# Attention and quantised feed-forward on one core: the second inverse root moved behind the head sums, squares per tile, part of the maximum taken early, bias row moved behind the first quantised tiles

## The reference, cut to what matters

```
n1  = layernorm(x)                       # inverse root of the variance: the first inverse root
q   = rope(n1 @ Wq), k = rope(ctx @ Wk), v = ctx @ Wv      # 16 query heads in 4 groups, 4 kv heads of 32
a   = mean over heads of softmax(q k / sqrt(32)) v
x1  = x + a @ Wo
n2  = layernorm(x1)                      # the second inverse root
i_scale = max(|n2|) / 127                # one number over all 64 batches
out = (clip(round(n2 / i_scale)) @ ternary(W).T) * w_scale * i_scale + bias
y   = x1 + out
```

## Time and profile before

| | |
|---|---|
| median of three runs | 1318.34 us (1316.42 to 1319.36) |
| profiled execution, its own time | 1320.26 us |
| its span, first to last instruction | 1318.4 us |
| mean granted TensorE clock | 0.989 |
| busy: PE, DVE, ACT, POOL | 96%, 89%, 78%, 60% of the span |
| first part, steady | about 150 to 950 us |
| change between the parts | about 950 to 978 us |
| second part | 978 us to the end |

### The profile page before, as it was taken

The page is one execution under the profiler, slowest core; times in us unless marked ns, Lnnn a source line. Parts: engine busy times, 40 slices in busy tenths (PEclk is TensorE's granted clock), DMA queues, the critical chain, the costliest instruction groups (busy, mean ns, idle before and its releaser), DMA issues.

```text
span 1318.4 us, 36698 instructions
## 1 busy us (share of the span) xinstructions
PE 1269.2 (96%) x9848; PEld 1087.7 (82%) x9911; DVE 1174.6 (89%) x2644; ACT 1026.7 (78%) x2338; POOL 794.8 (60%) x1536
## 2 busy tenths in 40 slices
PE   6897999999999999999999999999969999999998
PEld 5787999999999999999999999999935555555554
DVE  4876899999999999999999999999968888888887
ACT  3454788888888888888888888888857888888886
POOL 3564888888888888888888888888820000000000
PEclk9998999999999999999999999999979999999999
DMA  8674345465555555555555452322108999999945
GB/s 268 172 212 129 104 148 192 146 191 154 183 158 178 162 174 162 174 169 168 174 163 181 155 169 75 102 77 100 37 0 334 400 401 399 397 401 402 406 202 223
DMA packets 100815, 265.18 MB, mean 201 GB/s; under 512 B 49705, under 2 KB 65769, under 8 KB 72114
## 3 DMA queue, kind: packets, MB, share of 16 engines
q1 hardware_dynamic: 100786, 264.86, 58.5%
HBM read 139.64 MB, written 125.17 MB: 201 GB/s over the span
## 4 chain that ended last, share of the span: by engine, by line
PE 86%; DVE 6%; DMA 3%; issue 2%; SPq 1%; ACT 1%; POOL 1%; DVEq 0%; POOLq 0%; ACTq 0%
PE bank L1245 18%; PE bank L1165 17%; PE bank L1213 13%; PE bank L1135 8%; PE bank L1200 8%; PE bank L1186 6%; PE bank L1236 4%; PE bank L1176 4%; PE bank L1243 3%; PE bank L1155 2%; PE bank L1147 2%; DMA x_sb<-in_ctx 1%; PE bank L1062 1%; DMA k_scr<-x_sb 1%; DVE cT_parts L752 1%
## 5 line engine op out<-in xcount | busy, mean ns | idle before, releaser
L1245 PE MATMUL bank<-wT,x_sb 128*128 128x512 f16 x1024 | 263.9, 380 | 3.5 <-issue 0.2
L1165 PE MATMUL bank<-wqs,xT_sb 128*128 128x128 f32 x2048 | 260.8, 281 | 0.4 <-ACT xT_sb L639 0.3
L717 ACT ACTIVATE x_sb<-bank,mean,cols 128x512 f32<-128x512 f32 x256 | 196.2, 775 | 67.5 <-PE bank L1245 67.3
L1165 PEld LDWEIGHTS bank<-wqs,xT_sb 128*128 128x128 f32 x2048 | 239.1, 192 | 7.1 <-ACT xT_sb L639 0.7
L1213 PE MATMUL bank<-v_blk,pT_sb 103*128 103x136 f32 x1536 | 199.0, 279 | 0.3 <-ACT pT_sb L681 0.3
L927 DVE SCALAR_TENSOR_TENSOR x_sb<-x_sb,mv_sb,bank 128x512 f32 (+1 forms) x256 | 180.0, 745 | 14.9 <-PE bank L1176 5.1
L1213 PEld LDWEIGHTS bank<-v_blk,pT_sb 103*128 103x128 f32 x1536 | 190.6, 190 | 0.5 <-ACT pT_sb L681 0.5
L1245 PEld LDWEIGHTS bank<-wT,x_sb 128*128 128x128 f16 x1024 | 100.6, 98 | 106.8 <-issue 1.7
L690 ACT ACTIVATE sq_sb<-x_sb 128x512 bf16 (+1 forms) x256 | 161.6, 631 | 18.7 <-DVE x_sb L927 1.4
L897 DVE TENSOR_REDUCE amax<-x_sb (+1 forms) x128 | 156.0, 1219 | 21.5 <-DVE bn_sb L888 6.3
L1002 DVE TENSOR_TENSOR x_sb<-x_sb 128x512 f32 (+1 forms) x256 | 164.8, 685 | 1.2 <-ACT x_sb L717 1.2
(11 more groups left out here) (125 smaller groups left out, 2566.8 us busy)
## 6 DMA issues: line engine op xcount, KB each, us to landing
out_y<-x_sb SPq DMA_DIRECT2D x112, 1024.0 KB, 7.2
x_sb<-in_x SPq DMA_DIRECT2D x64, 1024.0 KB, 6.4
x_sb<-out_y SPq DMA_DIRECT2D x48, 1024.0 KB, 9.1
x_sb<-in_ctx SPq DMA_DIRECT2D x38, 256.0 KB, 2.8
k_blk<-k_scr SPq DMA_DIRECT2D x256, 19.2 KB, 5.5
k_scr<-x_sb SPq DMA_DIRECT2D x38, 128.0 KB, 2.3
v_scr<-x_sb SPq DMA_DIRECT2D x38, 68.0 KB, 2.4
v_blk<-v_scr SPq DMA_DIRECT2D x128, 10.2 KB
```

The lines of the kernel that those rows point to most:

```text
L717: act.activation(u_sb[:, t, :], bank[4 + t][:, :], ACT.Identity, bias=stat_of(mean1, j, t, back), scale=cols[:, 6:7]).then_inc(scaled_t, 1)
L1165: last = pe.matmul(bank[2][:, t * HD:(t + 1) * HD], xT_sb[:, t, c, :], wqs[:, c, :], start=c == 0, stop=c == EC - 1)
L1245: last = pe.matmul(bank[4 + t][:, :], q16T_sb[:, t, c, :], wT[:, c, :], start=False, stop=c == EC - 1)
```

## The change

Five edits. On POOL the second inverse root goes from the head of the step to behind the mean (L538), ahead of the rope. On ACT each square waits for its own tile of the residual alone. On DVE the variance always waits for the inverse root two pairs back, so that its double buffer is free. The product and maximum over the first 248 of 256 columns are taken in the step that holds the last residual, and only eight columns and the earlier result remain for the end. The bias row is made behind the first two tiles that DVE quantises instead of ahead of them (the helper functions move with it; they are unchanged).

```diff
+HELD = 4
+        st_b = x_sb[:, 2, 1, 0:1 + 2 * HELD]
+        ahead_done = sem("ahead_done")
@@ gpsimd step
-                if rstd:
-                    j, kj, gj = rstd
-                    pool.wait_ge(var_ready, j + 1)
-                    pool.tensor_tensor(rs2[...2 * j...], ve2_sb[...], mhalf[:, :], ALU.pow).then_inc(rs2_ready, 1)
                 if head:
...
                     pool.tensor_tensor(mean1[:, bass.ds(2 * j, 2)], o_sb[:, :, D], mv_sb[:, kj, :, 0],
                                        ALU.add).then_inc(mean_ready, 1)
+                if rstd:
+                    j, kj, gj = rstd
+                    pool.wait_ge(var_ready, j + 1)
+                    pool.tensor_tensor(rs2[...2 * j...], ve2_sb[...], mhalf[:, :], ALU.pow).then_inc(rs2_ready, 1)
                 if proj:
@@ scalar step
                     j, kj, gj = stat
-                    act.wait_ge(added_t, 2 * j + 2)
                     for t in range(2):
+                        act.wait_ge(added_t, 2 * j + t + 1)
                         at_least(act, sq_done, 2 * j + t)
@@ vector step
                     j, kj, gj = rstd
-                    if not resid:
-                        dve.wait_ge(rs2_ready, j - 1)
+                    at_least(dve, rs2_ready, j - 1)
                     dve.wait_ge(sq_done, 2 * j + 2)
...
+                if isinstance(i, int) and i == NP_ + RESID - 1:
+                    ahead = NT - 2 * HELD
+                    dve.wait_ge(amax_done, NP_ - HELD)
+                    dve.wait_ge(rs2_ready, NP_ - HELD)
+                    dve.tensor_tensor(st_a[:, 0:ahead], amax[:, 0:ahead], rs2[:, 0:ahead], ALU.mult).then_inc(ahead_done, 1)
+                    dve.wait_ge(ahead_done, 1)
+                    dve.tensor_reduce(st_b[:, 0:1], st_a[:, 0:ahead], AX.X, ALU.max).then_inc(ahead_done, 1)
                 if resid:
@@ vector, between the parts
             dve.wait_ge(amax_done, NP_)
+            dve.wait_ge(ahead_done, 2)
             dve.wait_ge(rs2_ready, NP_)
-            mids(dve.tensor_tensor(st_a, amax[:, :], rs2[:, :], ALU.mult))
-            dve.tensor_reduce(cols[:, 2:3], st_a, AX.X, ALU.max).then_inc(scale_T, 1)
+            mids(dve.tensor_tensor(st_b[:, 1:], amax[:, ahead:], rs2[:, ahead:], ALU.mult))
+            dve.tensor_reduce(cols[:, 2:3], st_b, AX.X, ALU.max).then_inc(scale_T, 1)
...
             dve.wait_ge(mid, done[0])
+            dve.wait_ge(scale_ready, 1)
+            quantise(0, 0, False)
 ...
-            quantise(0, 0, False)
             unoffset(0, 0)
```

More of the change, by code:

```diff
@@ L498, in step @@
                 proj, score, value, head, resid, stat, rstd = (stage(i, k, g, lag) for lag in range(RSTD + 1))
-                if rstd:
-                    j, kj, gj = rstd
-                    pool.wait_ge(var_ready, j + 1)
-                    pool.tensor_tensor(rs2[:, bass.ds(2 * j, 2)], ve2_sb[:, kj % 2, :], mhalf[:, :], ALU.pow)\
-                        .then_inc(rs2_ready, 1)
                 if head:
@@ L539, in step @@
                                        ALU.add).then_inc(mean_ready, 1)
+                if rstd:
+                    j, kj, gj = rstd
+                    pool.wait_ge(var_ready, j + 1)
+                    pool.tensor_tensor(rs2[:, bass.ds(2 * j, 2)], ve2_sb[:, kj % 2, :], mhalf[:, :], ALU.pow)\
+                        .then_inc(rs2_ready, 1)
                 if proj:
@@ L1028, in _ @@
             quantise(0, 0, False)
+            a, a1, a2, part, row = (cols[0:BR, 3:4], rcol[:, 6:7], rcol[:, 7:8], a16[:, :], rcol[:, 3:4])
+            mids(dve.reciprocal(a, cols[0:BR, 6:7]))
+            mids(dve.tensor_copy(part, a))
+            mids(dve.tensor_tensor(a1, a, part, ALU.subtract))
+            mids(dve.tensor_scalar(row, part, rcol[:, 0:1], None, ALU.mult))
+            mids(dve.tensor_copy(part, a1))
+            mids(dve.tensor_tensor(a2, a1, part, ALU.subtract))
+            mids(dve.scalar_tensor_tensor(out=row, in0=part, scalar=rcol[:, 1:2], in1=row,
+                                          op0=ALU.mult, op1=ALU.add))
+            mids(dve.scalar_tensor_tensor(out=row, in0=a2, scalar=rcol[:, 2:3], in1=row,
+                                          op0=ALU.mult, op1=ALU.add))
+            dve.tensor_scalar(bones[0:BR, :], ones_sb[0:BR, :], row, None, ALU.mult).then_inc(bias_ready, 1)
             unoffset(0, 0)
```

## The result

The changed kernel takes 1345.3 us (median of 6 runs, 1344.28 to 1346.27), the kernel before 1319.8 us beside it (6 runs, 1316.42 to 1321.31). The ratio is 1.0195, with a 95% interval of 1.0185 to 1.0206: 2% slower. I had forecast 1318.0 us, no change, in a range of 1315.3 to 1322.0, with 0.20 for slower.

A forecast was written before the change was run, and what follows sets the result against it. PE was taken to bound the steady pairs and a chain across engines the drain; +0.3 + 0.60 - 0.25 - 0.36 - 0.46 - 0.12 = -0.29 us took 1318.34 to 1318.0 us, range 1315.3 to 1322.0.

The forecast's parts named there:

- the one on the steady pairs: Steady pairs: POOL's moved power ends the rope 0.60 us later, PE's idle absorbs it; +0.3 us in all.
- its upper bound of +6: Steady pairs: up to 0.1 us over the margin, paid once in two pairs over 119 pairs, +6 us.
- the loop closes: Rival, steady pairs: PE feels POOL's later rope in every pair; 1319.5 to 1323.7 us, middle 1321.3; chance 0.20.
- PE's spare 0.09 us at L1165: Steady pairs: PE stands still about 0.09 us per pair waiting for ACT, absorbing the late load with 0.04 to spare.
- PE idle ahead of L1147/L1160: Last loop step into the drain: PE waits for the later rope, +0.60 us; idle about 0.9 us there.
- last head product behind the reciprocal: Last head sums: POOL's head product starts 0.07 us after DVE's reciprocal, no longer held by the power; -0.25 us.
- early product and maximum: Drain, ahead of DVE's last residual: their 0.90 us is hidden in 1.33 us of idle, with 0.4 to spare.
- end of the residual to the last variance: Drain, squares per tile: the first square starts 0.7 us earlier, so DVE's last variance starts earlier; -0.36 us.
- last product and maximum: End of the first part: eight columns for 256 take 0.42 us instead of 0.88; -0.46 us.
- end of the scaling to PE's first bias product: Start of the second part: bias row behind the first quantised tiles starts PE's work earlier; -0.12 us, bounds -0.4 to +0.2.
- the third rival: Drain: PE's low clock level is left earlier or later, 1 to 1.5 us either way; chance 0.10.

The follow-up runs named there:

- e3: DVE's added wait for the inverse root alone, put on the kernel before: 1320.17 us, ratio 1.0002.
- e5: Changed kernel with the variance as a scalar_tensor_tensor that reads a tile of EPS as second input: 1344.36 us, ratio 1.0196 to the kernel before.
- e4: Changed kernel with POOL's power behind the rope, last in POOL's step: 1318.05 us, ratio 0.9986 to the kernel before.
- e6b: Changed kernel with the variance as two operations of one column each instead of one of two columns: 1323.06 us, ratio 1.0027 to the kernel before.
- e8: Changed kernel with DVE's variance behind the reciprocal instead of two places ahead of it: 1318.8 us, ratio 0.9998 to the kernel before.
- e2: Changed kernel with POOL's power put back ahead of the head product, all other edits kept: 1319.3 us, ratio 0.9997 to the kernel before.
- e1: Kernel before with only the power moved behind the head sums and the DVE wait it needs: 1346.79 us, ratio 1.0201.
- e9: Changed kernel, power back ahead of the head product, plus an unused 240-column product behind the rope on POOL: 1324.85 us, ratio 1.0045 to the kernel before.

## Why the prediction was wrong, step by step

**The step that failed** is the one on the steady pairs, in the bounds of its DVE part. I wrote that L937 "runs without a gap to L885, that lets L509 go", and took its 2.41 us as fixed, with 0.05 to 0.1 for a register wait. The wait cost nothing (e3). The variance inside that stretch grew by 0.2 to 0.5 us in the steady pairs (median 0.160 to 0.648). What I left out was that moving the power takes away POOL's idle at just the moment of the variance. So the prediction had no term for the measured +25.7 us at all: its upper bound of +6 came from a wait that cost nothing and from another loop. (That bound was also added up short: 0.03 and 0.1 over make 0.13, which gives 7.7 us.) A prediction of a moved step has to ask what the engine beside it does *now* in that interval. I asked only who waits for whom.

The trace of before showed it, in two places that I did not use. DVE's L917, of the same form on two columns, lasts 0.31 us and ends at 601.50, and is as long in most of the trace (0.28 to 0.34 in 108 of 128 pairs, 0.16 where no instruction of POOL runs beside it):

```profile
601.19 0.31 DVE L917 TENSOR_SCALAR ve_sb<-mv_sb 128x2 f32<-128x2 f32 x1
```

beside POOL:

```profile
601.06 0.42 POOL L529 TENSOR_TENSOR ost_sb<-pw_sb 128x128 fp32r<-128x128 f32 x1
```

which ends at 601.48. And the variance itself has 430 ns as its longest, once, where its median is 160. It ends 0.02 us behind POOL's L535 there. An operation whose shortest and longest times differ twofold at one shape is a sign to look at what runs beside it.

I had not weighed the page that bears on it. The Trainium skill, "SBUF — State Buffer", Who interferes with whom, says that VectorE and GpSimd share one pair of ports as an exclusive lock, for VectorE's `tensor_scalar` in a two-port mode and for its instructions with two SBUF inputs beside a GpSimd instruction that reads SBUF, and that the second to issue is blocked until the first is done. The runs agree on the wait to the end of the running instruction (0.02 to 0.03 us behind it) and on both forms (`tensor_scalar` in the kernel after, two inputs in e5). The port itself is seen in no trace; only its name is taken from the Trainium skill. The runs differ from it in one point: beside the power of two columns, which takes 0.70 us and reads the same memory, the variance is not blocked (e4, 0.153 to 0.178 us).

**The rival "the loop closes"** had the right engine and sign, and the wrong loop and size: at most +6 us by a loop over two pairs that runs through PE. With the blocked variance out of the way 1.0027 remains, 3.6 us (e6b), within those bounds, though I had put +0.3 for it. In e8 nothing remains. The loop that was measured is another, of one pair, from the rope's end over the variance to the head product.

**PE's spare 0.09 us at L1165** was there and was used up: in the kernel after, L1178's loads follow L1168's by the natural 0.22 (600.39 to 600.61), not held by ACT.

**The drain.** Kernel after, DVE around the last pair:

```profile
993.33 0.41 DVE L926 TENSOR_TENSOR x_sb<-amax,rs 128x248 f32<-128x248 f32 x1
993.77 0.41 DVE L928 TENSOR_REDUCE x_sb<-x_sb 128x1 f32<-128x248 f32 x1
994.10 1.40 DVE L937 SCALAR_TENSOR_TENSOR x_sb<-x_sb,mv_sb,bank 128x512 f32<-128x512 f32 x2
...
996.66 0.16 DVE L876 TENSOR_SCALAR ve_sb<-ssq 128x2 f32<-128x2 f32 x1
997.72 0.17 DVE L971 TENSOR_TENSOR x_sb<-amax,rs 128x8 f32<-128x8 f32 x1 [0.90 <-POOL rs L541]
997.92 0.16 DVE L972 TENSOR_REDUCE cols<-x_sb 128x1 f32<-128x9 f32 x1
```

PE, the end of the first part and the start of the second:

```profile
979.02 0.44 PE L1160 MATMUL bank<-ident,qa_sb 128*128 128x128 f32 x2 [0.94 <-POOL qa_sb L556]
...
993.20 0.74 PE L1189 MATMUL bank<-wst,oT_sb 128*128 128x512 f32 x2 [0.47 <-ACT oT_sb L661]
...
1002.02 1.89 PE L1249 MATMUL bank<-ident,x_sb 128*128 128x128 f16 x16 [2.33 <-ACT x_sb L710]
1004.14 0.59 PE L1256 MATMUL bank<-brow,bones 128*128 128x512 bf16 x1 [0.24 <-DVE x_sb L993]
```

| step | forecast | measured in the kernel after |
|---|---|---|
| PE idle ahead of L1147/L1160 | 0.9 us | 0.94 |
| last head product behind the reciprocal | -0.25 | -0.23 (0.32 to 0.09) |
| early product and maximum | hidden, 0.4 to spare | 0.1 late: PE's result was there at 993.94, L937 starts at 994.10 |
| end of the residual to the last variance | -0.36 | -0.46 (1.62 to 1.16) |
| last product and maximum | -0.46 | -0.52 (0.88 to 0.36) |
| end of the scaling to PE's first bias product | -0.12 | +0.07 (3.48 to 3.55; the 3.48 rests on my place for an unrecorded product) |

The sixteen transposes L1249 run without a gap and PE then waits for L993, as forecast. So the drain was right in its mechanisms but for the bias row, which came out a loss. I had put the wait ahead of the first quantised tile at 0.05. From the start of the scaling to the start of what follows it was 0.26 us before (974.44 to 974.70), and is 0.45 now (1000.25 to 1000.70, L984 to L1011): 0.19 for the wait. From the last rope to the end the profile of e2 has 365.5 us and the kernel before 367.1, yet the timed ratio of e2 is 0.9997 (0.9987 to 1.0007), 0.4 us with 1.3 either way. PE's lower clock (0.50 granted) lasted 17.1 us there in the kernel before and in e3, 13.7 in e2, e4, e8 and the kernel after; it lasted 13.7 in e1 too, which has none of the other edits of the drain, and there the same stretch is 365.7 us. In e3, which has none either, it lasted 17.1 and the stretch is 367.4. So most of the profiles' 1.6 us goes with the clock and not with the edits, which is the mechanism of the third rival. How often it falls so in timed runs stays open.

## What to carry to other kernels

Before an instruction is moved on GpSimd, look at what VectorE does in the interval that becomes busy. Here a two-column `tensor_scalar`, and the same with two inputs, waited for the end of GpSimd's running sum or product of 128 to 256 columns. If what stands behind that operation releases GpSimd's next work, the two engines form a loop of GpSimd's whole work plus the way back (here 5.97 + 0.81 us). An idle stretch that looks free may be the window in which the other engine gets through. Two cures cost nothing here: the small VectorE operation behind the one that GpSimd waits for (e8, 0.9998), or GpSimd's two-column power at the place where the variance falls (e4, 0.9986).

## What the runs showed of the hardware that I had not expected

- The block depends on whether VectorE's operation has one column or two: two columns 0.648 us in the median, one column twice 0.20 us together, beside the same rope of 256 columns. A distance of four elements between the two columns changes nothing (0.648).
- GpSimd's power on two columns (0.70 us) does not block a two-column `tensor_scalar`, a 256-column sum (0.73 us) and a 240-column product (0.70 us) do. Whether this is the width or the operation stays open.
- A waiting VectorE operation is let in at the end of the running GpSimd instruction, though the next follows without a gap: it ended 0.02 us behind the first (599.94 against 599.92, e9).
